# An AdaLN attention and feed-forward layer on one core: other orders in the group loop, the last two groups written out, and a reordered opening

## The reference, cut to what matters

```python
xn = ln(x, g_norm)
q = (xn @ Wq).reshape(b, n, HEADS, DIM_HEAD).transpose(0, 2, 1, 3)
k, v = split(xn @ Wkv)                      # 64 each, shared by all heads; null k, v put in front
q = l2norm(q) * q_scale;  k = l2norm(k) * k_scale
sim = einsum('bhid,bjd->bhij', q, k) * SCALE + bias          # bias: 3-layer MLP of i - j
attn = softmax(where(causal | ~mask, neg, sim))
y = ln(einsum('bhij,bjd->bhid', attn, v) @ Wout, g_out)
xq = act_fake_quant(y);  gate, up = xq @ wq8(w_gate).T, xq @ wq8(w_up).T
out = x + act_fake_quant(silu(gate) * up) @ wq8(w_down).T    # scales: absolute maximum of the whole tensor
```

## Time and profile before

| | us |
|---|---|
| median of 3 runs | 302.04 (300.73 to 302.70) |
| the profiled execution, its time | 302.66 |
| its span | 300.9 |
| opening, to TensorE's first scores (L855) | 26.87 |
| 30 groups, to 239.2 | 212.3 |
| groups 30, 31 and the draining, to the last normalising of y (L1250) | 26.5 |
| from there to the end | 35.2 |

### The profile page before, as it was taken

How to read it: one execution, slowest core, us unless ns; L and a number is a source line. 1 busy time by engine, 2 the same in 40 slices (tenths; PEclk the granted TensorE clock), 3 DMA queues, 4 the chain that set the end, 5 groups by cost and what they waited for, 6 DMA issues and landing times.

```text
span 300.9 us, 7310 instructions
## 1 busy us (share of the span) xinstructions
PE 259.3 (86%) x2161; PEld 204.1 (68%) x2162; DVE 237.3 (79%) x965; ACT 228.0 (76%) x785; POOL 204.0 (68%) x394
## 2 busy tenths in 40 slices
PE   0769899989999999999999999999999987875260
PEld 0427778877787888778788878888787865761050
DVE  2758887887888888879887988787876767559993
ACT  1555989978987888888789978998888877249480
POOL 2277888788788779878987898778877755013301
PEclk9989999999999999999999999999999999899756
DMA  4279000000000000000000000000000020000013
GB/s 140 49 183 268 2 1 2 1 3 2 1 2 1 3 1 2 0 3 1 2 0 4 3 0 2 0 4 0 2 2 3 2 72 1 2 0 1 0 36 110
DMA packets 13083, 6.89 MB, mean 23 GB/s; under 512 B 1953, under 2 KB 12913, under 8 KB 13042
## 3 DMA queue, kind: packets, MB, share of 16 engines
q1 hardware_dynamic: 11874, 6.03, 7.5%
q10 hardware_dynamic: 1168, 0.36, 0.5%
HBM read 5.31 MB, written 1.07 MB: 21 GB/s over the span
## 4 chain that ended last, share of the span: by engine, by line
PE 63%; DVE 16%; POOL 5%; ACT 5%; issue 4%; DMA 3%; SPq 1%; POOLq 0%; DVEq 0%; ACTq 0%
PE bank L874 13%; PE bank L829 10%; PE front L855 7%; PE back L917 7%; PE front L917 5%; PE bank L718 5%; PE back L855 5%; PE bank L734 4%; DMA g1b<-in_L_cond_g_dram 3%; ACT prob L576 2%; DVE score L1227 2%; POOL prob L443 2%; DVE hmax L1360 2%; DVE oT L1217 2%; DVE oT L1396 2%
## 5 line engine op out<-in xcount | busy, mean ns | idle before, releaser
L576 ACT ACTIVATE prob<-score,negmax 128x258 f32<-128x258 f32 (+1 forms) x256 | 113.5, 450 | 30.5 <-DVE negmax L1227 30.5
L443 POOL TENSOR_SCALAR prob<-prob,rrow 128x258 f32<-128x258 f32 x254 | 107.3, 441 | 23.0 <-DVE rrow L1235 19.7
L396 POOL TENSOR_TENSOR rq<-qn,neghalf 128x8 f32<-128x8 f32 x32 | 53.3, 1666 | 2.7
L874 PE MATMUL bank<-pT,val 128*64 128x256 f32 (+1 forms) x512 | 49.7, 337 | 0.6 <-ACT pT L586 0.6
L576 ACT ACTIVATION_READ_ACCUMULATOR prob<-score,negmax 128x1 f32 x256 | 49.1, 192 | 0.0
L874 PEld LDWEIGHTS bank<-pT,val 128*64 128x64 f32 x512 | 32.2, 138 | 20.7 <-ACT pT L586 10.7
L829 PE MATMUL bank<-wout,oT 128*128 128x128 f32 x256 | 36.8, 287 | 5.4 <-DVE oT L1217 4.7
L1227 DVE CUSTOM_DVE_ANT_0 score<-back,bias 128x258 f32<-128x258 f32 (+1 forms) x128 | 38.0, 353 | 0.1
L1227 DVE CUSTOM_DVE_ANT_0 score<-front,bias 128x258 f32<-128x258 f32 (+1 forms) x128 | 37.8, 351 | 0.0
L829 PEld LDWEIGHTS bank<-wout,oT 128*128 128x128 f32 x256 | 31.0, 191 | 10.0 <-DVE oT L1217 6.9
L1096 DVE TENSOR_REDUCE qn<-sq 128x8 f32<-128x512 f32 x32 | 21.9, 685 | 19.6 <-ACT sq L522 19.0
(11 more groups left out here) (199 smaller groups left out, 458.3 us busy)
## 6 DMA issues: line engine op xcount, KB each, us to landing
bias<-relative_table SPq DMA_DIRECT2D x8, 256.0 KB, 5.0
out_dram<-prob SPq DMA_DIRECT2D x4, 256.0 KB, 3.1
X<-in_x_dram SPq DMA_DIRECT2D x1, 896.0 KB, 13.3
prob<-in_L_cond_Wq_dram SPq DMA_DIRECT2D x1, 512.0 KB, 5.9
wout<-in_L_cond_Wout_dram SPq DMA_DIRECT2D x1, 512.0 KB, 14.5
prob<-in_L_ffn_w_down_dram SPq DMA_DIRECT2D x1, 176.0 KB, 2.4
X<-in_x_dram SPq DMA_DIRECT2D x1, 128.0 KB, 4.1
prob<-in_L_ffn_w_gate_dram SPq DMA_DIRECT2D x1, 128.0 KB, 2.1
```

The costliest lines, as they stand in the source:

```text
L396: pool.tensor_tensor(dst, src, neghalf[:, 0:width], ALU.pow).then_inc(done, 1)
L443: pool.tensor_scalar(prob[:, par, h, cols], prob[:, par, h, cols], rrow[:, par, h, t:t + 1], 1.0, ALU.mult, ALU.mult).then_inc(normed, 1)
L576: act.activation(prob[:, par, h, cols], score[:, h % 4, cols], ACT.Exp, scale=-1.0, bias=negmax[:, par, h, t:t + 1], accum_out=rowsum[:, p ...
L874: last = pe.matmul(ps[a * D:a * D + D, pair * N + i0:pair * N + N], val[m % 2][:, blk, :], pT[:, 2 * pair + a, c0:c1], start=blk == 1, sto ...
```

## The change

It reorders work on every engine; the arithmetic is the same. In the opening, b1 and g1 are loaded from ScalarE's queue, after w1; forty fillers stand at TensorE's head, others between its waits; the third quarter of q goes ahead of the second MLP turn, two squares of q ahead of the second Silu; ScalarE's mask copy and VectorE's mask minimum go later; GpSimd's memsets go first; and x of batch 1 and the third quarter of q are normalised among group 0's scores. In the loop, kv is copied before pT copies 2 and 3, `k_normalise` and the old group's `invert` go behind the first `score_pair`, and x's statistics and power go one group earlier. The loop now ends at `LOOP = 30`; groups 30 and 31 and the draining are an `ending` on each engine, with a second buffer `pTe`, filled by VectorE, for group 30's transposed probabilities.

```diff
+LOOP = GB * B - 2
 def over_groups(group):
-    for at in range(GB * B + 2):
+    for at in range(LOOP):
...
-        q_ps0 = [bank[i] for i in (5, 2, 3, 4)]
+        q_ps0 = [bank[i] for i in (5, 2, 4, 5)]
...
@@ SyncE, then ScalarE (after w1s)
-            for dst, src in ((b1b[:, :], row(b1)), (g1b[:, :], row(g1))):
-                sp.dma_start(dst, src).then_inc(ld_mlp, 16)
+            for dst, src in ((b1b[:, :], row(b1)), (g1b[:, :], row(g1))):
+                act.dma_start(dst, src).then_inc(ld_mlp, 16)
@@ GpSimd, group and ending
+                if s.g == 3 and s.b + 3 < B:
+                    x_power(s.b + 3)
                 if s.quarter is not None and s.quarter >= 4:
                     q_power(s.quarter, s.quarter % 4)
...
-                if s.g == 0 and s.prev is not None and s.b + 2 < B:
-                    x_power(s.b + 2)
...
+            def ending():
+                y_power(B - 2)
+                normalise(heads(LOOP - 1)[2:4])
+                for at in (LOOP, LOOP + 1):
+                    normalise(heads(at)[0:2])
+                    normalise(heads(at)[2:4] if at == LOOP else heads(at)[2:3])
+                y_power(B - 1)
@@ ScalarE, opening
+            kv_evac(0, halves(misc))
+            q_square(0, q_ps0[0])
+            q_square(1, q_ps0[1])
+            mlp_silu(1)
+            mlp_turned(1)
+            q_square(2, q_ps0[2])
...
@@ ScalarE, group: kv before pT 2 and 3; ending
+                if s.kv is not None:
+                    kv_evac(s.kv, front_tails)
                 if s.turned is not None:
                     pT_evac(s.turned, 2)
                     pT_evac(s.turned, 3)
...
+                for i in range(4):
+                    exponent(heads(LOOP + 1)[i])
+                yT_evac(B - 2)
+                for i in range(4):
+                    pT_evac(LOOP + 1, i)
+                null_evac(B - 1)
...
@@ TensorE, opening
+                keep_busy(3, qT_ps)
                 pe.wait_ge(mlp_a, 2 * layer + 2)
...
             pe.wait_ge(consts, 3)
+            keep_busy(40, qT_ps)
...
             q_make_first(1)
+            q_make_first(2)
             mlp_turn(1)
...
-            pe.wait_ge(min_ready, 1)
-            least = pe.value_load(mask_min[:, :])
...
-            q_make_first(2)
+            keep_busy(6, qT_ps)
             qT_make(0)
             q_make_first(3)
...
+            keep_busy(6, misc)
+            pe.wait_ge(min_ready, 1)
+            least = pe.value_load(mask_min[:, :])
@@ TensorE, ending
+                s = Group(LOOP)
+                first_scores(s, masked)
+                pe.wait_ge(pT_ready, GH * (LOOP - 1))
+                second_scores(s, masked)
+                values(LOOP - 2)
                 turn(s, 0)
                 turn(s, 1)
+                for pair in range(2):
+                    y_products(LOOP - 2, pair)
                 turn(s, 2)
                 turn(s, 3)
...
+                s = Group(LOOP + 1)
+                first_scores(s, masked)
+                pe.wait_ge(pT_ready, GH * LOOP)
+                second_scores(s, masked)
+                turn(s, 0)
+                turn(s, 1)
+                values(LOOP - 1)
+                turn(s, 2)
+                turn(s, 3)
+                for pair in range(2):
+                    y_products(LOOP - 1, pair)
...
+                s = Group(GB * B)
+                for i in range(4):
+                    turn(s, i)
                 pe.wait_ge(yT_ready, B - 1)
                 null_weights(s.null)
+                values(LOOP)
+                values(LOOP + 1)
...
@@ VectorE, opening
-            dve.tensor_reduce(mask_min[:, :], mask_u[:, :].bitcast(U16), AX.X, ALU.min).then_inc(min_ready, 1)
...
             q_normalise(0, 0, q_ps0[0])
+            dve.tensor_reduce(mask_min[:, :], mask_u[:, :].bitcast(U16), AX.X, ALU.min).then_inc(min_ready, 1)
...
             q_norm2(3, 3)
-            q_normalise(2, 2, q_ps0[2])
-            x_normalise(1)
@@ VectorE, group (new order)
+                score_pair(heads(s.at)[0:2])
+                if s.turned is not None:
                     invert(heads(s.turned)[2:4])
+                if s.kT is not None:
+                    k_normalise(s.kT)
+                if s.quarter >= 4:
                     q_normalise(s.quarter, s.quarter % 4, q_ps)
                 if s.at == 0:
+                    q_normalise(2, 2, q_ps0[2])
+                score_pair(heads(s.at)[2:4])
+                if s.at == 0:
+                    x_normalise(1)
                     qT_evac(2, 2, 0)
...
-                if s.g == 3 and s.b + 3 < B:
+                if s.g == 2 and s.b + 3 < B:
                     x_stats(s.b + 3)
@@ VectorE, ending
+            def pTe_copy(i):
+                dve.wait_ge(pT_done, heads(LOOP)[i][0] + 1)
+                dve.tensor_copy(pTe[:, i, :], bank[i][:, 0:3 * P]).then_inc(pTe_ready, 1)
+            def ending():
+                score_pair(heads(LOOP)[0:2])
+                invert(heads(LOOP - 1)[2:4])
+                score_pair(heads(LOOP)[2:4])
+                oT_copy(LOOP - 2)
+                y_normalise(B - 2)
+                invert(heads(LOOP)[0:2])
+                ffn_weights(0)
+                score_pair(heads(LOOP + 1)[0:2])
+                invert(heads(LOOP)[2:4])
+                score_pair(heads(LOOP + 1)[2:4])
+                pTe_copy(0)
+                pTe_copy(1)
+                invert(heads(LOOP + 1)[0:2])
+                oT_copy(LOOP - 1)
+                pTe_copy(2)
+                pTe_copy(3)
+                invert(heads(LOOP + 1)[2:4])
+                last_normalise()
+                yT_absmax(B - 3)
+                ffn_weights(1)
+                clip_scales()
+                oT_copy(LOOP)
+                ffn_weights(2)
+                oT_copy(LOOP + 1)
+                ffn_weights(3)
+                ffn_weights(4)
+                y_stats(B - 1)
```

More of the change, by code:

```diff
@@ L735, in qT_make, with keep_busy @@
                 last.then_inc(qT_done, 1)
+            def keep_busy(count, ps):
+                for _ in range(count):
+                    pe.transpose(ps[:, 0:P], ident[:, :], ident[:, :])
             def mlp_turn(layer):
@@ L742, in mlp_turn @@
                 last.then_inc(mlp_t, 1)
+                keep_busy(3, qT_ps)
                 pe.wait_ge(mlp_a, 2 * layer + 2)
-            def keep_busy(count, ps):
-                for _ in range(count):
-                    pe.transpose(ps[:, 0:P], ident[:, :], ident[:, :])
             pe.wait_ge(consts, 3)
+            keep_busy(40, qT_ps)
             for t in range(2):
@@ L1274, in group @@
             def group(s):
-                if s.quarter is not None and s.quarter >= 4:
+                if s.quarter >= 4:
                     q_norm2(s.quarter, s.quarter % 4)
-                if s.kT is not None:
-                    k_normalise(s.kT)
-                if s.turned == GB * B - 1:
-                    invert(heads(s.turned)[2:4])
-                    last_normalise()
                 if s.summed is not None:
```

162 lines of the change are left out of this document (72 added, 90 removed).

## The result

| | before | after |
|---|---|---|
| median | 301.84 (299.51 to 304.01, 20 runs) | 302.88 (301.54 to 305.27, 20 runs) |
| the profiled execution, its span | 302.66, 300.9 | 302.16, 300.4 |
| ratio of the two | | 1.0063, 95% interval 1.0041 to 1.0085 |

The forecast was 295.2. The changed kernel is no faster; by its interval it is 0.4 to 0.9% slower, where the forecast had 2.3% faster. The starts of TensorE's value products cut the execution into four pieces, and each can be set beside its step of the prediction. All times are relative to the profiled execution of the kernel before.

A forecast was written before the change was run, and what follows sets the result against it. TensorE, nearly always busy in the loop, waits on other engines in g = 1, the opening's chain runs over a load, and the ending's clock falls. Gains 1.7 (loop) + 1.7 (opening) + 3.4 (ending) = 6.8 us give 295.2; range 290.5 to 299.0.

The forecast's parts named there:

- Loop, g = 1, 2, 3: Loop groups: g = 1 gains 2.6 us, g = 3 gains 0.6, g = 2 loses 1.5; together 1.7 gained.
- Opening, the first score: Opening: the first score comes 3.5 us before 28.34, from 1.2 + 2.2 + 1.3 - 1.2.
- Opening, the loads: Opening: b1 and g1, on ScalarE's queue, land at 11.7 us, the middle of 9.5 and 13.8.
- Rival 5: Opening: the two loads land no earlier; opening gains 0.9 us, 296.0 in all; included in the forecast case's 0.60.
- Opening, the Silu: Opening: with two squares of q ahead of it, the layer's Silu comes at some 15.3 instead of 16.46 us.
- Opening, the third quarter: Opening: ahead of the second MLP turn it costs 1.0 us of TensorE's idle time and removes VectorE's 2.20 us wait.
- Opening, what is given back: After the first score: work waits for x of batch 1, normalised behind two score pairs; 1.7 us of gain is left.
- Ending: Last two groups, written out: the last normalising comes at 262.3 against 265.73, 3.4 us gained; bounds 1.0 and 5.1.
- Rival 1: Opening: the fillers don't raise the clock; it loses 0.6 us instead of winning 1.7, 297.5 in all; chance 0.13.
- Rival 2: Loop: the moves let the engines run ahead; gain 5.0 us in place of 1.7, 291.9 in all; chance 0.13.
- Rival 3: Ending: VectorE's extra copies and weight work limit the gain to 1.0 us, 297.6 in all; chance 0.10.
- Rival 4: Loop: normalising comes late in all 26 groups, 0.3 us each, 7.8 lost; 304.7 in all; chance 0.04.

The follow-up runs named there:

- c1: b1 with three loop repairs: reciprocal first in g = 2, batch 3's x power at group 3's end, group 2's keys scaled before the output copy; 295.72 us.
- a1: The changed kernel with the loads of b1 and g1 back on SyncE's queue; 301.94 us.
- a3: The changed kernel with b1 and g1 still on ScalarE's queue, but the two vcol loads moved to SyncE's; 301.63 us.
- c3: c2 with the product of the third quarter of q ahead of the second MLP turn on TensorE; 295.21 us.
- d1: c1 with x of batch 1 normalised behind both pairs of scores of group 0, as in the changed kernel; 299.28 us.
- b1: a1 with the third quarter of q and x of batch 1 normalised ahead of the first scores, as in the kernel before; 297.84 us.
- b3: The kernel before with only the new ending (groups 30, 31 and the draining); 298.44 us.
- d2: d1 with twenty identity transposes filling TensorE's wait ahead of the transposes of x of batch 1; 297.90 us.
- c2: c1's loop and ending with the opening of the kernel before; 295.70 us.
- d3: c1 with the third quarter of q normalised behind the first pair of scores of group 0, as in the changed kernel; 295.09 us.
- c4: c1 with b1 and g1 loaded from ScalarE's queue, as in the changed kernel; 295.96 us.
- a2: The kernel before with only the loads of b1 and g1 moved to ScalarE's queue; 302.77 us.
- b2: The changed kernel with the whole opening of the kernel before, on every engine; 297.68 us.
- b4: b2 with the reciprocal first in g = 2 and x of batch 3 at its old places in groups 3 and 4; 296.77 us.

## Why the prediction was wrong, step by step

**What bounds the kernel.** Right. The groups, their waits and the ending are where the prediction found them. What failed is the opening's term, and one piece of the loop's.

**Loop, g = 1, 2, 3.** Right, and nearly to the number: g = 1 wins 0.66 in the traces (predicted 0.5), g = 2 loses 0.25 (0.25 predicted, by the reciprocal, as GpSimd's wait shows), g = 3 wins nothing (0.1). Together -1.4 against -1.7.

**"The power of the next x moves into g = 3 ... nothing, with 0.1 us to spare."** This holds in full batches, and failed in batch 0. The step was read off one batch in the middle and applied to all; in the first batch kv, kT and xT come one group later, as the text on the code says. There the power stands ahead of q's (0.8 us in group 3), and the keys' scaling behind the first scores holds TensorE (0.5 us in group 2). It cost 1.6 us; c1 took 1.2 of it back.

**Opening, the first score.** This is the term that was mis-sized most: 3.5 us early in the sum, 1.0 late in the profile, 4.5 of the opening's miss of 4.9. a1 puts 2.3 us of it down to the moved loads with their blocked issue; the other 2.2 lie in the steps below, the Silu and the third quarter.

**Opening, the loads.** The landing was judged well (g1b landed 7.0 us after an issue at 3.17, thus at 10.2; I had 11.7). The failed step is the price of the issue: it was put at nothing on ScalarE. An engine that issues DMAs stands still while an issue waits, here 5.47 us for the last two, 4.33 for the last one alone. What decides that an issue waits, these runs do not show. The trace of the kernel before shows the effect already, on a queue behind which no compute stands: the issue of SyncE's last load in the opening takes 9.12 us, and the prediction did not look at it.

```profile
5.87 9.12 SPq L343 DMA_DIRECT2D wout<-in_L_cond_Wout_dram  x1
```

(The Trainium skill, "DMA: Bandwidth & Descriptors", "Issuing engines are not separate DMA queues", was weighed; from it the prediction worked out a landing near 13.8. The landing at 10.2 speaks against that working, not against the page's sentence that the loads interleave: the later loads of the same queue took 12.7 us for `ks` and 11.9 for `vcol`, where they had taken 11.2 and 11.0, so others paid for it.) Rival 5's condition, no earlier landing, did not come; its Silu "near 17.6" is what a1 has, with the loads back. The loads did land earlier, and nothing came of it.

**Opening, the Silu.** "At some 15.3": it came at 19.92, and at 17.11 (a3) and 17.61 (a1) without the block. The step did put ScalarE's second square behind VectorE's sum; it did not follow what stands ahead of that sum. That is the centring, which in a1 waits for g1b until 13.92, and the wait for the keys' loads, which in a3 ends at 15.56. Moving g1b ahead of `ks` in one queue only changes which of the two VectorE waits for.

**Opening, the third quarter.** Its square was to give 2.2 us; alone (c3) it takes 1.5 us off VectorE's wait, and 0.57 reach the first score.

**Opening, what is given back.** The sum had x of batch 1 behind two pairs of scores and let 1.8 us go. In the profile of the changed kernel it is 2.2, without a fall of the clock, so the mechanism was right; the third quarter's normalising (0.68 us), which now stands between the pairs, was left out of it. But where the clock falls in the wait it is 3.8 (a1): the prediction saw the wait and not what the clock can do in it. By the medians d1 against c1 puts this one line at 3.6 us and b1 against a1 the two at 4.1, more than the block's 0.9 (the changed kernel against a1, by the ratios). So of single repairs it is the one worth most.

**Ending.** Right: 3.9 against 3.4, alone as well (b3). Less the 3.4 us by which group 29 is late, TensorE's scores of group 31 stand at 245.88 (245.9 predicted), the turns end at 254.2 (254.2), and y is normalised at 261.8 (262.3). The clock's share in it was not measured apart.

**Rivals.** Rival 1 fell: the fillers raise the clock. (The Trainium skill, "TensorE: Matmul & The Clock Gate", "Part 4: PE-mode transpose", says transposes don't count as busy time in the same way. Here the forty transposes took the next ones from 0.66 to 0.44 us, in every trace that has them, and in d2 with twenty of them the granted clock was 1.00 where in d1 it was 0.61; the traces decide against the rule.) Rival 2 fell: the steady loop won 1.4 us and not 5.0. Rival 3 fell. Rival 4's mechanism, the late reciprocal, stayed in g = 2, as the forecast had it. No rival named the opening as the part that loses much: its bound was a loss of 0.6 us, from the clock alone, and no bound was set for the issuing or for the line with x.

**A version that beats both.** c1, c2, c3 and d3 have medians of 295.1 to 295.7 us, 1.6 to 2.0% below the kernel before: the new ending (3.9 us) and the new loop with its three repairs (2.4 us between groups 2 and 29), with x of batch 1 normalised before the first scores. That is near the 295.2 of the forecast, but on these chips the kernel before itself ran 1.2 us below the 302.04 that the forecast started from: the gain is 5.1 to 5.7 us of the 6.8. The opening has little share in it: c2, with the opening of the kernel before, has c1's median.

## What to carry to other kernels

Before a load is moved to a compute engine's queue, look in the trace at how long the last issues of a full queue stand: the same wait will hold the compute engine itself, and what it holds may be the head of the chain (or, as c4 shows, something covered). Follow also the loads that the moved one now stands in front of: here `ks` was waited for in place of g1b. A step that is read off a steady batch has to be followed once more through the first one, where the preparation runs a group later. And a wait that a move opens on TensorE can cost more than its length, because in four of five traces the products behind it ran slower; what that costs can be estimated by filling the wait with transposes that nobody reads.

## What the runs showed of the hardware

- ScalarE's issues: with nine loads 0.44 to 0.74 us each, 1.17 us for the last pair; with eleven 5.47, 5.33 and 4.87 us for the last pair, in the changed kernel, in a2 and in c4. SyncE's issue of Wout stands 9.12 us as the twelfth of its queue in the kernel before and 7.12 us as the tenth in the changed one.
- The same opening comes out 2.2 us apart in two executions, for the larger part by TensorE's clock. b2 and b4 share it to the line; VectorE's wait for g1b ends at 14.04 and 13.50, 0.5 us of it, the third quarter of q takes 1.92 us in the one and 1.02 in the other, and the first score stands at 28.90 and at 26.72:

```profile
21.38 1.92 PE L751 MATMUL back<-prob 128*128 128x512 f32 x2
```

```profile
20.10 1.02 PE L753 MATMUL back<-prob 128*128 128x512 f32 x2
```

  The kernel before ranges from 298.1 to 303.1 us over 19 runs on one chip. That this is the same effect is likely and was not shown.
